# A Mamba layer with its states on the partitions: tiles of four states by 32 channels, state sums one group behind the scans

## The reference

```python
for i in range(4):
    xs, z = split(x @ in_w.T)                         # 512 channels each
    xc = silu(cb + sum(xs shifted by k * cw[:, k]))   # k = 0..3, causal
    dt, Bm, Cm = split(xc @ xp_w.T, [16, 32])         # 16 + 16 + 16
    delta = softplus(dt @ dt_w.T + dt_b)
    h_t = h_{t-1} * exp(delta_t * A) + (delta_t * xc_t) * B_t   # 512 channels x 16 states
    y_t = sum over the 16 states of h_t * C_t, + xc_t * D_skip
    y = (y * silu(z)) @ out_w.T
    x = layer_norm(y + x) * ln_w + ln_b
```

## Time and profile before

| | |
|---|---|
| Median of 3 runs | 12,323.49 us (12,323.26 to 12,326.33) |
| The profiled execution | 12,305.88 us |
| Its span | 12,304.1 us |
| Instructions | 107,024 |
| Busy: DVE, PE, POOL, ACT | 11,095.7, 8,618.5, 7,372.0, 4,922.0 us |
| Granted TensorE clock, mean | 0.849 |
| First scan starts, last one ends | 164.2 us, 11,177.5 us |

### The profile page before, as it was taken

One profiled execution on the slowest core, in us unless ns is written; L12 is line 12 of the kernel. 1 busy time (PEld: TensorE's weight loads), 2 busy tenths in 40 slices (PEclk: granted clock), 3 DMA queues, 4 the chain that ended last, 5 costly groups with the idle time before them and its releaser, 6 DMA issues. The chain is left out here.

```text
span 12304.1 us, 107024 instructions
## 1 busy us (share of the span) xinstructions
PE 8618.5 (70%) x20260; PEld 3527.3 (29%) x20260; DVE 11095.7 (90%) x14024; ACT 4922.0 (40%) x6934; POOL 7372.0 (60%) x5182
## 2 busy tenths in 40 slices
PE   4767777777777777777777777777777777775566
PEld 1222222222222222222222222222222222222344
DVE  7999999999999999999999999999999999996555
ACT  3434443444434443444444443444344443442222
POOL 3666666666666666666666666666666666664222
PEclk9888888888888888888888888888888888887878
DMA  2011101110011101110011100110011100100000
GB/s 91 34 38 36 38 21 38 37 43 28 34 38 36 38 21 38 38 41 31 31 38 36 38 25 35 37 43 31 31 38 36 38 25 35 38 35 25 25 25 23
DMA packets 191635, 433.27 MB, mean 35 GB/s; under 512 B 10928, under 2 KB 155056, under 8 KB 157552
## 3 DMA queue, kind: packets, MB, share of 16 engines
q1 hardware_dynamic: 190960, 427.63, 9.8%
HBM read 375.15 MB, written 52.43 MB: 35 GB/s over the span
## 5 line engine op out<-in xcount | busy, mean ns | idle before, releaser
L632 POOL TENSOR_TENSOR hc<-h,c_all 128x512 f32<-128x512 f32 x4096 | 5833.3, 1426 | 3959.7 <-DVE h L711 2933.5
L711 DVE TENSOR_TENSOR_SCAN h<-dA,carry,bu 128x512 f32<-128x512 f32 x4032 | 5123.5, 1271 | 73.4 <-ACT dA L485 71.4
L485 ACT ACTIVATE dA<-delta,cur 128x512 f32<-128x512 f32 x4096 | 2866.1, 719 | 5566.7 <-DVE h L711 5436.8
L361 PE MATMUL acc<-hc,ident 128*128 128x512 f32 x8192 | 4988.2, 695 | 3.2 <-POOL hc L632 3.0
L351 PE MATMUL B_all<-bsp,sel 128*128 128x512 bf16 x4096 | 1809.0, 442 | 2851.1 <-DVE bu L699 2829.1
L699 DVE TENSOR_TENSOR bu<-du,B_all 128x512 f32<-128x512 f32 x4096 | 2825.9, 690 | 521.6 <-PE B_all L351 276.3
L351 PEld LDWEIGHTS B_all<-bsp,sel 128*128 128x128 bf16 x4096 | 412.1, 101 | 5960.9 <-DVE bu L699 5663.9
L361 PEld LDWEIGHTS acc<-hc,ident 128*128 128x128 f32 x8192 | 1830.6, 225 | 542.9 <-issue 304.7
L391 PE MATMUL work<-xT,inw 128*128 128x512 f32 x2048 | 1065.7, 647 | 1.4 <-DMA dtw<-in_dtw 1.4
L764 DVE SCALAR_TENSOR_TENSOR xc<-xs,cur,xc 128x512 f32<-128x512 f32 x768 | 786.3, 1024 | 0.4
L718 DVE TENSOR_SCALAR carry<-h,keep 128x4 f32<-128x4 f32 x1023 | 625.6, 612 | 2.0
(11 more groups left out here) (157 smaller groups left out, 6235.3 us busy)
## 6 DMA issues: line engine op xcount, KB each, us to landing
c_all<-c_dram SPq DMA_DIRECT2D x256, 1024.0 KB, 4.7
x_in<-xbuf SPq DMA_DIRECT2D x64, 512.0 KB, 6.0
x_res<-xbuf SPq DMA_DIRECT2D x64, 512.0 KB, 6.5
xbuf<-x_res SPq DMA_DIRECT2D x64, 512.0 KB, 2.9
n_x<-in_x SPq DMA_DIRECT2D x18, 512.0 KB, 3.4
f_xa<-in_x SPq DMA_DIRECT2D x17, 512.0 KB, 4.1
f_xm<-xbuf SPq DMA_DIRECT2D x17, 512.0 KB, 5.0
xbuf<-n_x SPq DMA_DIRECT2D x16, 512.0 KB, 2.9
```

Of the source, the lines that this page charges most:

```text
L361: pe.matmul(acc[q % 2][:], ident[:], hc[:, s % RING_HC, :], start=s == 0, stop=s == NS - 1, skip_group_check=True).then_inc(summed, 1)
L485: act.activation(dA[:, s % RING_DA, :], delta[:, p_, q, :], ACT.Exp, scale=cur[:, p_, C_A + NS * q + s:C_A + NS * q + s + 1]).then_inc(da_ ...
L632: pool.tensor_tensor(hc[:, s % RING_HC, :], h[:, s % RING_H, :], c_all[:, s, :], ALU.mult).then_inc(hc_ready, 1)
L711: dve.tensor_tensor_scan(h[:, s % RING_H, :], dA[:, s % RING_DA, :], bu[s % RING_BU][:], start, ALU.mult, ALU.add).then_inc(scanned, 1)
```

## The change

The Mamba stage is replaced by one with another tiling. A tile has 4 states by 32 channels on its 128 partitions. A turn has 16 groups (`NG`; four quarters `q` of 128 channels by four sets `j` of four states), and a group has four scans, one for each 32 channels of the quarter.

- delta and du = delta * xc are stored in DRAM and loaded back so that 32 channels stand four times on the partitions (`replicate`, `drep`, `durep`). C is loaded for four states at a time (`crep`).
- PE `broadcast_b` is one float32 matmul for a group. `times_b` is two DVE products of 128 x 2 x 512 for a group, in place of one of 128 x 512 for each scan. `times_c` on POOL is two products of 128 x 2 x 512.
- `sum_states` is four float32 matmuls with a 128 x 32 matrix, each into 32 partitions of one acc bank. `skip_term`, a matmul with a diagonal matrix, opens each quarter. The sums are placed at `s - 1`; the gates stand in the turns' steps 6, 10, 14 and, for the last quarter, in step 2 of the next turn.
- The convolution is four matmuls with diagonal matrices for each block of channels; `keep_states`, the halo, the parameters, 1 + tanh and the normalisation go to ACT; products for silu and the softplus to POOL, as are the variance and the Newton step. The residual is added on PE by a matmul with the identity. Mean and variance are made by bn_aggr.
- The state is no longer multiplied by `keep` at a sequence's start: the turn of phase 0 starts its scans with 0.0, so the loop has four turns in its body.
- The work ahead reaches two chunks: transposition, projection and convolution of chunk g + 2 stand in turn g.

The core of the diff:

```diff
-            def broadcast_b(at):
-                n, p_, q, s, U = at
-                pe.matmul(B_all[s % 2][:], sel[:, s, :], bsp[:, p_, :], start=True, stop=True).then_inc(bb_ready, 1)
+            def broadcast_b(at, p_):
+                n, s, G = at
+                if positive(G):
+                    pe.wait_ge(bu_ready, 2 * G)
+                pe.matmul(B_all[:], spread_b[:, s % QS, :], dtc[:, p_, :], start=True, stop=True).then_inc(bb_ready, 1)
+            def skip_term(n, p_, q):
+                if positive(DB * n + q):
+                    pe.wait_ge(acc_read, DB * n + q)
+                pe.matmul(acc[:], skip[:, q, :], xc[:, p_, q, :], start=True, stop=False, skip_group_check=True)
+            def sum_states(at, p_):
+                n, s, G = at
+                if s % QS == 0:
+                    skip_term(n, p_, s // QS)
+                for k in range(4):
+                    if k % 2 == 0:
+                        pe.wait_ge(hc_ready, 2 * G + k // 2 + 1)
+                    ins = pe.matmul(acc[32 * k:32 * k + 32, :], gather[:], hc[:, 4 * (s % 2) + k, :], start=False,
+                                    stop=s % QS == QS - 1, skip_group_check=True)
+                    if k % 2 == 1:
+                        ins.then_inc(summed, 1)
...
+            def turn(g, ph):                       # PE
+                for s in range(NG):
+                    broadcast_b(group(g, s + 1), here if s + 1 < NG else other)
+                    sum_states(group(g, s - 1), here if s >= 1 else other)
+                    if not is_last(g):
+                        if s == 0:
+                            convolve(nxt, 3)
+                        if s == 2:
+                            project_x(nxt, other)
+                        if s in (3, 4):
+                            project_dt(nxt, other, 2 * (s - 3))
+                            project_dt(nxt, other, 2 * (s - 3) + 1)
+                    if not is_first(g):
+                        if s in (5, 6):
+                            project_out(g - 1, other, s - 5)
+                    if not is_last(g):
+                        if s in (8, 9):
+                            project_in(nxt, 2 * (s - 8), 1)
+                            project_in(nxt, 2 * (s - 8) + 1, 1)
+                        if s == 10:
+                            transpose_x(g + 2)
+                        if s in (11, 12):
+                            project_in(g + 2, 2 * (s - 11), 0)
+                            project_in(g + 2, 2 * (s - 11) + 1, 0)
+                        if s in (13, 14, 15):
+                            convolve(g + 2, s - 13)
...
+            def times_c(at):                       # POOL
+                for k in range(2):
+                    pool.wait_ge(scanned, 4 * G + 2 * k + 2)
+                    if positive(2 * G + k - 3):
+                        pool.wait_ge(summed, 2 * G + k - 3)
+                    pair = slice(r + 2 * k, r + 2 * k + 2)
+                    pool.tensor_tensor(hc[:, pair, :], h[:, pair, :], crep[:, j:j + 1, :].to_broadcast([P, 2, T]),
+                                       ALU.mult).then_inc(hc_ready, 1)
...
+            def gate(n, p_, q):                    # DVE
+                dve.wait_ge(summed, 2 * (NG * n + QS * (q + 1)))
+                dve.tensor_tensor(sz[:, p_, q, :], acc[:], sz[:, p_, q, :], ALU.mult).then_inc(acc_read, 1)
...
+            def turn(g, ph):                       # DVE
+                for s in range(NG):
+                    at, nxt = group(g, s), group(g, s + 1)
+                    scan(at, ph, 0)
+                    if s == 2 and not is_first(g):
+                        gate(g - 1, other, DB - 1)
+                    if s in (6, 10, 14):
+                        gate(g, here, (s - 6) // 4)
+                    times_b(at, 1)
+                    scan(at, ph, 1)
+                    scan(at, ph, 2)
+                    times_b(nxt, 0)
+                    scan(at, ph, 3)
+                    if not is_first(g):
+                        if s == 8:
+                            statistics(g - 1)
+                        if s == 9:
+                            moments()
```

More of the change, by code:

```diff
@@ L180, in mamba_layers @@
[L180 to L189, removed]
@@ L212, in mamba_layers @@
[L212 to L219, removed]
+        in_w, mid_w, skip_w, post_w = sem("in_w"), sem("mid_w"), sem("skip_w"), sem("post_w")
@@ L231, in turns @@
             turn(0, 0)
[L232 to L245, removed]
+            turn(1, 1)
+            with eng.Fori(0, (TOT - 4) // 4) as i:
+                for r in range(2, 6):
+                    turn(4 * i + r, r % 4)
+            turn(TOT - 2, 2)
+            turn(TOT - 1, 3)
         def is_first(g):
@@ L426, in _ @@
-            for d in range(KD):
-                transpose_x(0, d)
+                        ins = pe.matmul(half, sz[:, p_, k, t * P:(t + 1) * P], outw[:, k, :], start=False, stop=k == DB - 1)
+                ins.then_inc(w_filled[j], 1)
+            pe.wait_ge(consts, 80)
+            transpose_x(0)
             for e in range(DB):
@@ new lines, in copy_xT, with set_halo @@
+            def copy_xT(n):
+                for d in range(KD):
+                    wait_filled(act, d, fill(d, n, "tr"))
+                    act.copy(xT[:, d, :], W[d][:]).then_inc(w_read[d], 1)
+            def set_halo(n, ph):
+                if positive(n):
+                    act.wait_ge(cubic, n)
+                if ph == 0:
+                    act.copy(xs[:, :, 0:3], zeros[:]).then_inc(halo_set, 1)
+                else:
+                    act.wait_ge(halo_kept, n)
+                    act.copy(xs[:, :, 0:3], halo[:]).then_inc(halo_set, 1)
@@ L679, in _, with turn @@
-            for e in range(DB):
-                for k in range(2):
-                    softplus(0, 0, e, k)
+            pool.wait_ge(set_up, 1)
+            silu_xc(0, 0)
+            for k in range(4):
+                softplus(0, 0, k)
+            def turn(g, ph):
+                other = 1 - ph % 2
+                for s in range(NG):
+                    if not is_last(g):
+                        if s == 2:
+                            silu_xc(g + 1, other)
+                        if s == 7:
+                            softplus(g + 1, other, 0)
+                    times_c(group(g, s))
+                    if not is_first(g):
+                        if s == 10:
+                            variance(g - 1)
+                        if s == 12:
+                            newton_step(g - 1)
+                    if not is_last(g):
+                        if s == 8:
+                            softplus(g + 1, other, 1)
+                        if s in (10, 11):
+                            softplus(g + 1, other, s - 8)
+                    if not is_first(g):
+                        if s == 15:
+                            affine(g - 1, 0)
+                            affine(g - 1, 1)
@@ new lines, in times_b, with scan @@
+                if positive(4 * G + 2 * k - 2):
+                    dve.wait_ge(scanned, 4 * G + 2 * k - 2)
+                dve.tensor_tensor(bu[:, 2 * k:2 * k + 2, :], durep[q % 2][:, 2 * k:2 * k + 2, :],
+                                  B_all[:].unsqueeze(1).to_broadcast([P, 2, T]), ALU.mult).then_inc(bu_ready, 1)
+            def scan(at, ph, k):
+                n, s, G = at
+                dve.wait_ge(da_ready, 4 * G + k + 1)
+                if k % 2 == 0:
+                    dve.wait_ge(bu_ready, 2 * G + k // 2 + 1)
+                    if positive(2 * G + k // 2 - 3):
+                        dve.wait_ge(hc_ready, 2 * G + k // 2 - 3)
+                if k == 0:
+                    if positive(G - 1):
+                        dve.wait_ge(carried, G - 1)
+                r, c = 4 * (s % 2) + k, 4 * s + k
+                start = 0.0 if ph == 0 else carry[:, c:c + 1]
+                dve.tensor_tensor_scan(h[:, r, :], dA[:, r, :], bu[:, k, :], start, ALU.mult, ALU.add).then_inc(scanned, 1)
@@ L888, in _ @@
-            turns(dve, turn)
-            gate(TOT - 1, 1, DB - 1)
-            for k in range(7):
-                finish(TOT - 1, k)
+                dve.wait_ge(a_step, 10)
+            for tile, value in ((minus_ln2, -LN2), (quad_bias, CUBIC[2]), (cubic_bias, CUBIC[1]), (quad_rest, CUBIC[3]), (one, 1.0),
+                                (c_eps, EPS), (c_half, 0.5), (c_minus, -1.0), (c_three, 1.5)):
+                dve.memset(tile[:], value)
+            dve.memset(zeros[:], 0.0).then_inc(set_up, 1)
@@ new lines, in _, with turn @@
+            work_out_a()
+            times_b(group(0, 0), 0)
+            def turn(g, ph):
+                here, other = ph % 2, 1 - ph % 2
+                for s in range(NG):
+                    at, nxt = group(g, s), group(g, s + 1)
[8 more added lines that the diff above has]
+                    times_b(nxt, 0)
+                    if s == 9 and not is_first(g):
+                        dve.wait_ge(stats, g)
+                    scan(at, ph, 3)
```

(11 more changed lines are left out.)

1021 lines of the change are left out of this document (522 added, 499 removed).

## The result

The changed kernel takes 10,014.2 us (10,010.8 to 10,018.3, 4 runs) against 12,324.9 us: the ratio is 0.812, with a 95% interval of 0.811 to 0.814. The forecast was 11,000 us with a range from 10,150 to 11,900.

A forecast was written before the change was run, and what follows sets the result against it. DVE was taken to bound the kernel, by instruction count and partly by meeting POOL. Outside work 1,293 us, lead-in and tail 30, and 64 chunks of 151 gave 10,987; with a median of 11,005, say 11,000 us, range 10,150 to 11,900.

The forecast's parts named there:

- the price of the four sums: PE's four sums into 32 of 128 partitions: bounds 3.41 and 0.85 us a group, carried at 3.41 and 2.13.
- the chain: PE waits at skip_term for DVE's gate, the next broadcast queued behind: four stalls, 29 or 25 us a chunk.
- the 8.5 us between the gates: Steps with extra PE matmuls outlast DVE's 6.98 us: 1.0 lost in seven steps, 1.8 in step 6, sums at 3.41.
- Floor: DVE's own work after the change, without stalls: 116 us a chunk, 124 with the dear product.
- the cold restarts between the gates: PE starting again at a low clock after idling, as in step 8: some 2 or 5 us a chunk.
- the dearer case: Sums one after the other at 3.41 us: 116 + 29 + 8.5 + 2 = 156 us a chunk.
- the case with sums at 2.13: Same floor, gates 25 us, nothing lost in the steps between, cold restarts some 5: 146 us a chunk.
- The count of 144 matmuls: PE's work a chunk in whole matmuls: 123 us at 2.4 GHz, 246 at 1.2, level with DVE.
- rival 2: PE is the bound at 1.2 GHz, idled by every gate: slower than before, up to 17,000 us; chance 0.11.
- a cheap chain: PE keeps 2.4 GHz, four sums cost 2.13 us, stalls 14: chunk 130 us, 9,660 us in all; chance 0.14.
- 3: Another feeder, POOL's bursts or du late, adds 5 to 12 us a chunk: 11,330 to 11,770 us; chance 0.13.

The follow-up runs named there:

- Experiment 3: Changed kernel with the four sums of a group as 128x128 matrices into all of acc, in place of 128x32 into 32 partitions: 10,872.9 us.
- experiment 2: Changed kernel with DVE's gates one step earlier (steps 5, 9, 13 and 1), sums still one group behind: 9,069.8 us.
- experiment 4: Changed kernel with PE doing the projection or convolution of steps 5, 9 and 13 before it waits for the gate: 9,095.2 us.
- experiment 1: Changed kernel with the sums two groups behind in place of one: 8,870.8 us.
- experiment 5: experiment 1 with the 16 copies a chunk of the last column (128x4) moved from ACT back to DVE: 10,078.4 us.
- experiment 7: Changed kernel with full-width sums and the sums two groups behind, together: 9,295.0 us.
- experiment 6: Kernel before the change with only the saving of the states' last columns moved from DVE to ACT: 12,198.4 us against 12,306.3.

## Why the prediction missed

**The step that failed is the price of the four sums.** The prediction bounded it by 3.41 us and 0.85 us, carried 3.41 and the middle, 2.13, and took the chunk between these two (156 and 146, hence 151). Measured are 1.06 us at the high level and 1.94 at the low one, next to the lower bound (0.85) that it had written down and then not carried as a case of its own with the chain. Put into the prediction's own sum for step 2, with the rows above: 0.77 + 2.00 (skip) + 1.87 (sums) + 1.95 (a broadcast at the low level, from its start to that of the next sums) - 4.1 = 2.5 us, measured 2.72; for step 6: 0.77 + 3.87 + 4.98 + 1.07 - 4.1 = 6.6, measured 6.57. Skip and sums took 3.87 us where the forecast had 6.8 or 5.7; a part of that gain is lost again, because the work behind them now stands in the low stretch of the clock (4.98 us for half of the output projection in place of 4.27, 1.95 for the broadcast of step 2 in place of 1.07). The stalls of this turn are 6.57, 6.14, 5.89 and 2.72, together 21.3 us, where the forecast had 29 or 25; and the 8.5 us between the gates are absent. Floor and stalls together give 114.1 + 21.3 = 135.4 us. Experiment 3 is the control: with the dearer sums, stalls of nearly the predicted size appear at the gates and between them.

**A second term failed: the cold restarts between the gates**, 2 us in the dearer case and 5 in the other. No row stood behind these figures, and in the changed kernel such restarts cost nothing: in step 8 PE begins again at 5025.90 after 4.48 us without work, its broadcast takes 1.73 us in place of 1.02, and DVE does not wait; DVE's only waits in this turn are the four at the gates. They do cost in experiments 2 and 4 (2.29 and 1.96 us in the instances above). In the case with sums at 2.13 (146 us a chunk, 10.6 too many) this term missed by 5 us, the stalls by 3.7 and the floor by 2; in the dearer one (156) the stalls by 7.7, the steps between by 8.5, restart and floor by 2 each.

The page on array tiling in the Trainium skill ("TensorEngine Tiling (Array Packing)", "Key Properties") has the tiles work in parallel, and the runs agree: 1.06 against 3.60 us for the same four sums. The weighing named it and then let the price of a middle stand for it. The other half of the rule, the drain at a change of mode, is small in the one pair of rows compared: the sums start 0.95 us after the broadcast (5013.03 to 5013.98), 0.09 more than the 0.86 between a broadcast at 5009.07 and full-width sums at 5009.93 in experiment 3. The change back was not measured.

**Right, point by point.** The gate chain: its four places, its order and what DVE waits for; experiments 1, 2 and 4 take it away in three ways and give 1,143, 944 and 919 us. DVE's floor: 116 us forecast, 114.1 measured, with the 1,024-column product at 1.13 us from start to start (1.12 between 5004.04 and 5005.16). The clock is at the low level when PE starts again behind the wait (granted share 0.50 from 5004.2 to 5009.0) and back at the high one by 5011. POOL: 105 to 115 us forecast, 103 measured, products of 2.36. ACT: about 90 forecast, 79 measured. The loads of delta and du are hidden: one wait of 98.6 us at the very start, none later. DVE's new stream does not wait for POOL; experiment 5 shows what one small copy in it would cost. The tail was +3 (forecast +5).

**Wrong besides.** The lead-in grew by 48 us (first scan at 212.6 in place of 164.2), not by 25. The count of 144 matmuls is 10 too high (experiment 7); it is not a term of the sum, and half of the projection was priced rightly as 10 half-wide ones, but it made PE look more loaded, and rival 2 nearer, than they were.

The rivals: 1 (a cheap chain, 130 us a chunk) rested on a clock that stays high with sums at 2.13; the clock fell at each gate and the sums were cheaper. The truth lay between it and the forecast, and the range, which took only a part of this rival in, ended 2 us a chunk too high. 2 and 3 did not occur. The change as a whole pays because DVE issues 41% fewer instructions (8,268 in place of 14,024) with half as many products, and others do what stood between the scans; placing the sums one group behind, with the gates where they are, costs 1,143 us of that: with two groups the kernel takes 8,871 us.

Open: in experiment 1 nine scans in all stand 6 us or so without a releaser that the profile shows (57.6 us). Those between 1,000 and 7,000 us are 471 us apart or a multiple of it, which is four chunks, one pass of the loop's body, and the one at 2801.08 is the first scan of a turn. So they seem to go with the loop's passes; what they wait for was not tried.

## What to carry to other kernels

When an engine works its queue in order, look for each pair of waits that face each other: the instruction that waits (here the skip term), what frees it (the gate), and everything queued behind the first that the second's engine needs next. Moving either by one step, or moving unrelated work from behind the wait to before it, took away 80 to 83% of what experiment 1 did (experiments 2 and 4). Where a price has two bounds far apart and one mechanism sits at each, carry each as a case instead of the middle. Moving a small operation to an idle engine pays only if that engine's queue has no long stretch in front of it (experiment 6).

## What the runs showed of the hardware

- Four float32 matmuls of 128 rows by 32 columns into the four partition quarters of one bank, eight records, take 1.06 us at the high clock level and 1.94 at the low one (the changed kernel, 5013.98 and 5006.18). As full-width matmuls they take 3.60 us at the high level (experiment 3, 5002.20), 3.4 times as long.
- A 128x4 TENSOR_SCALAR on DVE took 1,383 ns on average beside POOL products of 2.36 us, and the six looked at ended with a POOL instruction (experiment 5). Products with one operand in PSUM took 1,212 ns on average beside the same POOL work (the changed kernel).
- Scans that start from the constant 0.0 take 1,204 ns, scans that start from a saved column 1,264 (1,024 and 3,072 of them).
